# Attention scores of a decoder layer from 96 stacked rows of two heads, laid by transfers within SBUF, in place of masked keys

## What is computed

```python
q = jnp.einsum('bsd,hde->bhse', x, wq) + bq          # 16 heads of 16 features
k = jnp.einsum('bsd,hde->bhse', x, wk) + bk
scores = jax.nn.softmax(jnp.einsum('bhse,bhte->bhst', q, k) * scale, axis=-1)
att = jnp.einsum('bhst,bhte->bhse', scores, v)
```

## Time and profile before

| | |
|---|---|
| median of 3 runs | 1063.31 us |
| profiled execution, its own time | 1064.93 us |
| its span, first to last instruction | 1063.2 us |
| TensorE busy | 946.8 us, 89% of the span |
| VectorE busy | 757.0 us, 71% |
| ScalarE busy | 696.2 us, 65% |
| GpSimd busy | 99.1 us, 9% |
| transfers | 86.40 MB, 81 GB/s over the span |
| granted TensorE clock, mean | 0.956 |

### The profile page before, as it was taken

The page is one execution under the profiler, slowest core; times in us unless marked ns, Lnnn a source line. Parts: engine busy times, 40 slices in busy tenths (PEclk is TensorE's granted clock), DMA queues, the critical chain, the costliest instruction groups (busy, mean ns, idle before and its releaser), DMA issues.

```text
span 1063.2 us, 17552 instructions
## 1 busy us (share of the span) xinstructions
PE 946.8 (89%) x6480; PEld 850.4 (80%) x6480; DVE 757.0 (71%) x1526; ACT 696.2 (65%) x1231; POOL 99.1 (9%) x117
## 2 busy tenths in 40 slices
PE   6558687988799989999899989999899999999997
PEld 5447687878688878888798878988798888989997
DVE  6757768786688757787678758786678757655675
ACT  6347675665567766667677666677676665656775
POOL 2012001100120011100111001100011001000000
PEclk9669998999899999999999999999899999999999
DMA  6022233222122222222222222221222222232360
GB/s 200 11 70 89 90 109 100 80 60 70 51 80 71 79 70 80 67 83 80 70 90 70 71 90 63 69 88 61 79 80 80 61 69 80 87 112 90 103 186 11
DMA packets 89268, 86.40 MB, mean 81 GB/s; under 512 B 5960, under 2 KB 89184, under 8 KB 89184
## 3 DMA queue, kind: packets, MB, share of 16 engines
q1 hardware_dynamic: 89184, 85.29, 26.1%
HBM read 83.17 MB, written 2.10 MB: 80 GB/s over the span
## 4 chain that ended last, share of the span: by engine, by line
PE 65%; DVE 19%; ACT 11%; issue 4%; DMA 0%; POOL 0%; SPq 0%; ACTq 0%; POOLq 0%; DVEq 0%
PE up_ps L407 9%; PE up_ps L409 9%; PE up_ps L408 9%; PE down_ps L615 9%; PE down_ps L616 8%; PE down_ps L617 8%; DVE w_lo L790 4%; PE bank L407 3%; PE bank L408 3%; PE bank L409 3%; DVE h_lo L790 2%; ACT probs L674 2%; DVE pt_lo L870 2%; ACT L674 2%; DVE kd L820 1%
## 5 line engine op out<-in xcount | busy, mean ns | idle before, releaser
L728 ACT ACTIVATE h_all<-up_ps,b_all 128x512 f32<-128x512 f32 (+1 forms) x296 | 182.7, 632 | 292.6 <-PE up_ps L409 291.1
L615 PE MATMUL down_ps<-w_hi,h_hi 128*128 128x256 f32 x1024 | 299.9, 293 | 41.4 <-DVE h_lo L790 41.4
L790 DVE TENSOR_TENSOR w_lo<-w_raw,w_hi 128x512 fp32r<-128x512 f32 x296 | 206.1, 710 | 153.2 <-ACT w_hi L739 153.0
L616 PE MATMUL down_ps<-w_lo,h_hi 128*128 128x256 f32 x1024 | 293.7, 287 | 0.0
L617 PE MATMUL down_ps<-w_hi,h_lo 128*128 128x256 f32 x1024 | 293.6, 287 | 0.0
L615 PEld LDWEIGHTS down_ps<-w_hi,h_hi 128*128 128x128 f32 x1024 | 199.2, 194 | 54.1 <-DVE w_lo L790 39.7
L407 PE MATMUL up_ps<-x2t_hi,w_hi 128*128 128x512 f32 (+1 forms) x592 | 224.9, 380 | 0.0
L408 PE MATMUL up_ps<-x2t_lo,w_hi 128*128 128x512 f32 (+1 forms) x592 | 219.5, 371 | 0.0
L409 PE MATMUL up_ps<-x2t_hi,w_lo 128*128 128x512 f32 (+1 forms) x592 | 219.2, 370 | 0.0
L616 PEld LDWEIGHTS down_ps<-w_lo,h_hi 128*128 128x128 f32 x1024 | 200.0, 195 | 5.2
L790 DVE TENSOR_TENSOR h_lo<-h_all,h_hi 128x512 fp32r<-128x512 f32 x256 | 182.3, 712 | 27.6 <-ACT h_hi L719 27.6
(11 more groups left out here) (171 smaller groups left out, 1118.2 us busy)
## 6 DMA issues: line engine op xcount, KB each, us to landing
w_raw<-in_w_dram SPq DMA_DIRECT2D x296, 256.0 KB, 2.7
x_in<-in_x_dram SPq DMA_DIRECT2D x8, 256.0 KB, 3.0
ctx_sb<-in_ctx_dram SPq DMA_DIRECT2D x8, 256.0 KB, 3.1
out_dram<-acc SPq DMA_DIRECT2D x8, 256.0 KB, 3.2
w_raw<-in_wq_dram SPq DMA_DIRECT2D x1, 256.0 KB, 3.0
w_raw<-in_wk_dram SPq DMA_DIRECT2D x1, 256.0 KB, 4.2
w_raw<-in_wv_dram SPq DMA_DIRECT2D x1, 256.0 KB, 4.3
w_raw<-in_wo_dram SPq DMA_DIRECT2D x1, 256.0 KB, 4.6
```

Source lines behind the costliest of these rows:

```text
L615: nc.tensor.matmul(ps, hi, w2h[:, c, :], start=c == 0 and j == 0, stop=False, skip_group_check=True)
L616: nc.tensor.matmul(ps, hi, w2l[:, c, :], start=False, stop=False, skip_group_check=True)
L728: a = nc.scalar.activation(h_all[:, unit % HALL, k * wide:(k + 1) * wide], up_ps[unit % 2][:, k * wide:(k + 1) * wide], ACT.Gelu_apprx_tan ...
L790: return nc.vector.tensor_tensor(dst, src, hi.bitcast(F32), ALU.subtract)
```

## The change

The three products of a score group become one that sums over 96 partitions. For two heads (32 features) three blocks of 32 partitions are stacked: `k_stack` has high, low and high keys, `q_stack` high, high and low queries, so that one product over 96 partitions gives the sum of the three. The two heads are kept apart by columns: the 256 columns are the keys of head a on its own 16 partitions of each block, and zero elsewhere, for a = 0 and 1. GpSimd sets `k_stack` to zero once; the transfers write the same places in every pair. `HC // 2 = 4` pairs of heads, two chunks and two sequences make 16 products of 256 columns.

The stacks are filled by transfers within SBUF on SP's stream (`stack`), at step 4 and, for pair 0, ahead of the last four early weight loads: 24 of 16 partitions for the keys, 12 of 32 partitions for the queries, each with both chunks and both sequences. TensorE waits for all 36 (`stacked`) before the first scores of a pair; SP's own waits are for the low keys, the low queries, and the end of the earlier pair's scores. `head_mask`, `kd`, `diagonal` and ScalarE's copies of pair 0 are gone. The full keys and queries now lie in `att` and `y1`, which are free by then.

```diff
@@ sync
+            def stack(p):
+                if first(p):
+                    sp.wait_ge(stacks_clear, 1)
+                else:
+                    sp.wait_ge(scores_ps, QUADS * p)
+                sp.wait_ge(k_rest_ready, p + 1)
+                for g in range(HC // 2):
+                    for i, t in enumerate((k_hi, k_lo, k_hi)):
+                        for a in range(2):
+                            sp.dma_start(k_stack[i * TWO + a * DH:i * TWO + (a + 1) * DH, :, g, a, :].bitcast(F32),
+                                         t[g * TWO + a * DH:g * TWO + (a + 1) * DH].bitcast(F32)).then_inc(stacked, 16)
+                sp.wait_ge(q_ready, p + 1)
+                for g in range(HC // 2):
+                    for i, t in enumerate((q_hi, q_hi, q_lo)):
+                        sp.dma_start(q_stack[i * TWO:(i + 1) * TWO, :, g, :].bitcast(F32), t[g * TWO:(g + 1) * TWO].bitcast(F32)).then_inc(stacked, 16)
...
                     for p, s in steps(FIRST_ITEM[n] + k):
+                        if s == STACK_STEP and p < NPAIR:
+                            stack(p)
@@ tensor, scores
                 rows = slice(j * S, (j + 1) * S)
+                if u == 0:
+                    pe.wait_ge(stacked, STACKED * (p + 1))
...
-                    keys_hi, keys_lo = keys(p, c, j, slice(i * HQ, (i + 1) * HQ))
-                    product(by_head(score_banks(p, u)[i]), q_hi[:, c, rows], q_lo[:, c, rows],
-                            keys_hi, keys_lo).then_inc(scores_ps, 1)
+                    for g in (2 * i, 2 * i + 1):
+                        mm = nc.tensor.matmul(by_head(score_banks(p, u)[i])[:, 2 * (g % 2):2 * (g % 2) + 2, :], q_stack[:, c, g, rows],
+                                              k_stack[:, c, g, :, rows], start=True, stop=True)
+                    mm.then_inc(scores_ps, 1)
@@ vector
-                for h in (2 * part, 2 * part + 1):
-                    i = nc.vector.tensor_scalar(kd[:, :, :, h, :], k_both[:, :, c, :].rearrange("p a (j t) -> p a j t", j=PAIR),
-                                                head_mask[:, h:h + 1], None, ALU.mult)
@@ gpsimd
+            nc.gpsimd.memset(k_stack[:].bitcast(F32), 0.0).then_inc(stacks_clear, 1)
```

More of the change, by code:

```diff
@@ L35, in decoder_layer @@
     VW = DH + 1
+    TWO = 2 * DH
     QUADS = PAIR * C * 2
@@ L310, in score_banks @@
             return (bank, up_ps, down_ps, up_ps)[u] if first(p) else bank
[L312 to L319, removed]
+        STACKED = 16 * 3 * (HC // 2) * 3
         def values_by_head(t):
@@ L377, in _ @@
                 load_piece(m)
+            stack(0)
             sp.wait_ge(proj_ready, 4)
@@ L439, in scores @@
                 for i in range(2):
-                    if u == 0 or u == 2 and not first(p):
-                        pe.wait_ge(kd_ready, i + 1 if first(p) else 2 * C * p + (2 * c + i - 1))
                     if u % 2 and not first(p):
@@ L648, in attend @@
                     act.wait_ge(k_ps, p + 1)
-                    for dst in (k_both[:, 0], k_hi):
+                    for dst in (k_all, k_hi):
                         for c in range(C):
@@ L660, in attend @@
                     a.then_inc(q_hi_ready, 1)
-                    if first(p):
-                        act.wait_ge(masks_made, MASKS)
-                        act.wait_ge(k_rest_ready, 1)
-                        for h in range(HC):
-                            for part, t in enumerate(first_keys):
-                                a = nc.scalar.activation(t[:, :, h, :], k_both[:, part, 1, :].rearrange("p (j t) -> p j t", j=PAIR),
-                                                         ACT.Copy, scale=head_mask[:, h:h + 1])
-                        a.then_inc(first_keys_ready, 1)
                 for u in range(UNITS):
@@ L810, in norm @@
                 return i
-            def diagonal(p, c, part):
-                if c == 0 and part == 0:
-                    dve.wait_ge(k_rest_ready, p + 1)
-                if c > 0 and part == 0:
-                    dve.wait_ge(scores_ps, QUADS * p + 2 * PAIR * c)
-                for h in (2 * part, 2 * part + 1):
-                    i = nc.vector.tensor_scalar(kd[:, :, :, h, :], k_both[:, :, c, :].rearrange("p a (j t) -> p a j t", j=PAIR),
-                                                head_mask[:, h:h + 1], None, ALU.mult)
-                if h % HQ == HQ - 1:
-                    i.then_inc(kd_ready, 1)
             def scan(i, state, inc):
@@ L837, in attend @@
                     dve.wait_ge(k_hi_ready, p + 1)
-                    low(k_both[:, 1], k_both[:, 0], k_hi[:]).then_inc(k_rest_ready, 1)
+                    low(k_lo[:], k_all, k_hi[:]).then_inc(k_rest_ready, 1)
                     dve.wait_ge(q_hi_ready, p + 1)
-                    low(q_lo[:], q_all[:], q_hi[:]).then_inc(q_ready, 1)
-                for c in range(C):
-                    for part in range(HC // 2):
-                        if s == DIAGONAL_STEP[c][part] and not (first(p) and c == 1):
-                            diagonal(p, c, part)
+                    low(q_lo[:], q_all, q_hi[:]).then_inc(q_ready, 1)
                 if s == V_STEP:
@@ L1166 @@
                + list(range(ATT_STEP, ROUTE_STEP[-1] + 1)))
-MASKS = 6
+MASKS = 3
 DVE_SETUP = 6
```

33 lines of the change are left out of this document (12 added, 21 removed).

## The result

The changed kernel takes 1215.39 us, the median of four runs (1212.69 to 1217.23); the kernel before, run beside it, 1062.80 (1061.29 to 1063.31). The ratio is 1.1436 [1.1411, 1.1462]: 14% slower. The prediction had the direction and the mechanism, but said 1154 us, and the time lies 13 us above the range's upper end of 1202.

The account below looks back on a forecast made before the run. TensorE, busy 89% of the span, was taken as the bound: 1064.9 + 104 (waits) + 14 (clock) - 22 (products) - 5 (masks) = 1156 us profiled, 1154 us as median; range 1118 to 1202.

Parts of the forecast that it names:

- the price of an issue: SP's queue, 36 transfers per pair: 0.45 us each, ends 0.36 and 0.51, bounded from loads.
- The wait for the transfers: TensorE before each pair's first scores: about 13 us, eight times, +104 us in all, with nothing caught up.
- the last of the signs that would have shown the prediction wrong: A later gap in a pair, as the one of 3.46 us, gone because other engines used the wait.
- The landing: After the last transfer's issue begins: 2.1 us until its data are there, ends 1.6 and 2.7.
- The beginning of the block: SP's issues start at the low keys' end; in pairs 1 and 2 behind a weight load, at 83.8 and 197.8.
- The products: Scores on TensorE: 24 x 0.232 us become 16 x 0.12 per pair, -22 us, ends 0 to -29.
- The clock: TensorE at half clock behind the waits of seven pairs, 2.0 us lost each: +14 us, ends 7 and 24.
- The cover of the weight loads: Weight loads delayed 16 us behind SP's issues: twelve slots give 33 and 43 us of lead, so no cost.
- The rival of starved loads: With half the lead, each pair waits about 4 us for weights, 30 us in all: 1184 us; chance 3%.
- Transfers one after another through few partitions: Stack transfers take 0.8 us each, more than an issue, 12.2 us more per pair: 1252 us; chance 12%.
- Faster: SP issues within SBUF so short that all 36 fit into 4.8 us, no wait: about 1034 us; chance 3%.
- The rule on small transfers: Skill's advice to merge transfers below 64 KB: calls the 24 key transfers badly cut, gives no other sum.

Follow-up runs that it names:

- the probe: Kernel before, with seven blocks of unused transfers behind its last store; SP's steady issue 0.636 us within SBUF, 0.466 from DRAM; GpSimd's 0.495.
- the last kernel: Changed kernel with transfers on two queues (SP 16 high-key, GpSimd other 20), begun early, and first two score units four steps later: 1111.79 us, ratio 1.0447.

## Why the prediction was wrong, step by step

**The step that failed is the price of an issue**: "I take 0.45, ends 0.36 and 0.51". It measured 0.636, outside both ends. All rows from which the ends came, are of transfers out of DRAM, and they were read as bounds by the number of rows that a transfer has; the upper end was even set below the highest of them, 0.53. By itself, with the same shape, a transfer from DRAM does cost 0.466, and one within SBUF 0.636 (0.63 to 0.68 in the four shapes tried). "No row shows a transfer within SBUF" stood in the prediction; but only the shape was bounded, and the route was not: the upper end should have lain well above the highest row. 35 x 0.186 x 8 = 52 us. With it the sum is 1206 us.

**The other 9 us.** Measured as the way from the low keys to the first scores, the prediction's own times make 112 us of shift (13.7, 16.3, 16.5 and 5 x 13.1), 8 more than at the maxima that it summed. At the right pitch that is 112 + 52 = 164; 168.3 were measured. Of the 4 us, 1 is pair 6's (a wait of 20.78 where pairs 3 to 5 have 19.9). All else was then to be 1156 - 1064.9 - 112 = 21 us shorter and is 17.9 shorter (3 us, of which the clock is 2.6). The last 1.6 is that the median of the four runs equals the profiled execution's time, where 1.6 less was assumed.

**Right, with their numbers.**
- The wait for the transfers is eightfold, it stands on TensorE, and next to nothing uses it: VectorE was idle behind it too (182.3 us before `neg_max`), and only in pairs 1 and 2 some 6 us were caught up. The gaps of 3.45 us that stand later in pairs are still there, five before and five after, so the last of the signs that would have shown the prediction wrong did not appear.
- The landing: 2.1 taken, 2.0 measured, for 16 partitions as for 32.
- The beginning of the block, at the end of the low keys in pairs 3 to 7 (505.41 after 505.01), and behind a weight load in pair 1.
- The products: 0.12 us apart; 96 partitions are not cheaper than 128. The gain without the fills is 27 us, as summed.
- The clock: 14 us forecast, 16.6 measured: 3.0 to 6.4 us of work at half speed cost 1.5 to 3.2 each, where 2.0 was taken.
- The cover of the weight loads: in the changed kernel no product and no rounding of the experts' weights waits for a load of them. The rival of starved loads did not occur.

**The rivals.** Transfers one after another through few partitions: refuted for one queue by the landing of 2.0 us and by the eight-fold larger transfer at nearly the same issue price. With two queues landings do grow (2.8 and 3.5 us at the median), which the changed kernel, with one, doesn't meet. It had the higher time on its side, and its 12% might have been read as leaving room above 1202; but it is another cause, and the room belonged to the issue's price. Faster: it needed 0.19 us an issue; the cheapest row within SBUF is GpSimd's 0.495.

**The rule on small transfers.** 32 KB and 256 KB within SBUF cost 0.65 and 0.68 us of SP's time: the issue doesn't go with the size. The Trainium skill, "DMA: Bandwidth & Descriptors", section "Rules for kernel authors", says to merge small transfers, since they pay mostly overhead. It spoke against the change: it gave no other sum, but its direction was the one in which the sum was off.

**The range.** It was built from the ends of the rows, as if a kind of transfer that no row shows must lie between those that are shown. Of its four uncertain terms (the gain, the issue, the landing, the clock) all but the issue came out inside their ends. Two ends were not worked out from rows: the clock's lower one, 7 us, is 1 us a fall where the text's own floor is 1.7; and the range's upper one comes out at 1200, not 1202, from the terms that are named.

## What to carry over

Before a change lays data out by many small transfers, count issues times the price of one on the queue that issues them, add one landing, and compare that with the time between the last of the source data and the first use. Bytes and partitions hardly mattered for the issue, but the route did (0.636 us within SBUF, 0.466 from DRAM). With a second queue look at the landings again: they grew from 2.0 to as much as 6.5 us. A transfer in a shared queue begins when the one ahead of it does, and each engine that gets the issues has instructions on which the others wait, so ask who stands behind them before moving work over. And cover that is won by moving work later has to be paid from the same schedule: here a gap of 4.93 us and a second fall of the clock took back all that it gave.

## What the hardware showed that was not expected

- SP's issue of a transfer within SBUF takes 0.636 us, and ScalarE's 0.644, where the same shape from DRAM takes 0.466; 8, 16, 32 and 128 partitions, one run or two, 16 to 256 KB change it by no more than 0.05.
- GpSimd issues the same transfer in 0.495 us, and the queries' transfers of 64 KB in 0.52. Where GpSimd issued the queries beside SP's keys, they landed after 2.6 us at the median, against 2.0 on SP's queue alone. That is not GpSimd's doing by itself: in the probe, with nothing beside them, its transfers of 32 KB landed after 1.8 us, and SP's own landings grew too while both issued (to 3.2 us in pair 4, back to 2.0 once GpSimd had finished).
- A wait of 20 us cost no longer a stretch at half clock than 3.0 to 6.4 us of work, where a wait of 3.46 us had cost 3.3. Gaps of 4.93 us cost nearly as much each as those of 20 (3.3 to 6.4 us of work at half clock behind the five in the last kernel), so here two short gaps cost the clock more than one long one.
